# A two-layer kernel on one core: x loaded first, the first gates ahead of the ternary pieces, and the second layer's statistics and inputs moved into the end of the first stage

## The chip, the cores and the metric

One core of one Trainium2 chip. The metric is the device time of one execution in microseconds (us), the median of several runs.

## The reference, cut to what matters

```python
x = L0_attn_x                                   # [2, 512, 256] f32
xn = _layernorm(x)
x = x + _L0_attn_ref(xn, ...) + _L0_ffn_ref(xn, ...)   # gated delta rule, 16 key heads, 32 value heads; ternary SiLU FFN
xn = _layernorm(x)
x = x + _L1_attn_ref(xn, ...) + _L1_ffn_ref(xn, ...)   # attention with 8 experts; GELU FFN, weights -1/0/1 by a threshold
```

In `_L0_attn_ref`, `x @ W_ba` gives beta = sigmoid(b) and g = -exp(A_log) * softplus(a + dt_bias); the products q, k, v go through a four-tap convolution and SiLU, and a rule over chunks of 64 tokens with decays exp(g_i - g_j). `_L0_ffn_ref` rounds its weights to bf16, makes them ternary in groups of 64, and divides the hidden values by their root mean square. `_L1_ffn_ref` compares its weights with 0.7 of their mean magnitude. `_L1_attn_ref` begins with an RMS norm with a weight, the q, k, v products and rotary tables.

## The kernel before, in words

The kernel has four stages with a barrier of all engines between them (`stage_end`, whose waits have line 63): `gdn` (the whole first layer), `layer1_in` (second layer: norm, q, k, v, rotation, and the second FFN's hidden values), `attention` and `experts`.

**The order of the work** in `gdn` is written out by hand. Every engine merges small generators; each yields a due time before a piece of work, and `in_order` issues the pieces by due time, sequentially on the engine. The 16 key heads are turns, 69.84 us apart (`TURN`), and turn 0 has a table of its own, `FIRST`, the last turn `FINAL`; `START` holds the due times of what is done once. Due times set only the order: an engine blocks at a piece whose semaphore isn't there yet, with all that is queued behind it.

**The start.** SyncE's queue issues, by `START`: the first weights `wqk` (2 DMAs, L491), one ternary input A (1 MB, L1176), x (2 DMAs of 512 KB into `yacc`, L174), wv, wz, wo (L496 to L505), then the other two ternary inputs (vn, og). `prep` makes constants, the statistics of x and xn on VectorE (L217 to L228), turns xn tile by tile on TensorE (L272) through two PSUM banks, ScalarE copies each tile out (L308, two copies per tile), and TensorE multiplies by W_ba (L278). VectorE and ScalarE then make the gates (L237 to L261; an Exp, a Ln and a Sigmoid, which each have an activation table of their own), which go to DRAM and back as rows GL and GR (L180, L482). From these TensorE makes the exponents of the decays (L559), ScalarE their exponentials E (L800), and GpSimd multiplies E by a factor `nsk` per token (L1129); VectorE multiplies the key scores by it into CM (L985), CM goes to DRAM and back, and VectorE begins the inverse (L1029).

**The ternary pieces** of the first FFN are six groups g of 128 x 1024: ScalarE casts to bf16 (`act_cast`, L1184), takes the magnitude (L1197) and the sign (L1203); VectorE sums by 64 (L1212) and compares (L1217); GpSimd does four operations (L1227 to L1235); TensorE turns the result (L1247), ScalarE copies it and writes it to DRAM.

**The end of stage one.** Turn 15 lies beside the first FFN: 16 hidden pieces, high and low parts of each for the down product (L1427, L1434), the down product on TensorE (L1388, four token tiles for each half b of the tokens). Between the halves stand 16 one-column products, which sum the squares (L1377), and TensorE waits for VectorE to read them (L1477). The four pieces of the second FFN's weights are compared (L1297, L1302) into one bf16 tile, so each compare waits until TensorE has turned the one before (L1318); ScalarE copies each and writes it to DRAM (L1327 to L1332). VectorE adds the down product to `yacc` at the very end (L1483).

**Stage two** (`layer1_in`) loads its weights and tables on SyncE and ScalarE after the barrier, makes statistics (L1584, L1588), GpSimd the inverse root (L1758), VectorE xn (L1594), TensorE turns xn through two banks (L1537) and multiplies by `wqkv` (L1702), which GpSimd has first scaled by the norm's weight (L1762). VectorE's rotation (L1605) waits for tables that GpSimd scales (L1774) after the DMAs. The hidden products (L1691) wait for parts of x from GpSimd (L1778, L1781); ScalarE's Gelu is L1679.

## Time and profile before

| what | value |
|---|---|
| median of 3 runs | 1536.25 us (1524.79 to 1536.82) |
| the profiled execution | 1536.63 us, span 1534.9 us |
| TensorE busy | 1378.7 us (90%) |
| VectorE, ScalarE, GpSimd busy | 69%, 57%, 35% |
| first stage ends, second begins | 1246.5 us |
| mean granted clock of TensorE | 0.962 |

The page cuts the span into 40 slices of 38.4 us. A timeline gives the start of each operation in us from the span's start, its duration, engine, line and operation, and in brackets how long its engine had been idle and what ended that. "<-issue" means that nothing in the profile explains the wait. L-numbers are lines of the kernel before. Several like instructions in a row are one line, with their count after "x" and their whole time.

### The profile page before, as it was taken

The page shows a single profiled execution, that of the slowest core. Times are in us where ns is not written, and L with a number is a line of the kernel's source. Part 1 is how long each engine was busy: PE and PEld are TensorE (multiplying, and loading weights), DVE is VectorE, ACT ScalarE, POOL GpSimd, SP SyncE. Part 2 cuts the span into 40 slices and gives each one's busy share as a digit, 9 for nine tenths or more (in the row PEclk, how much of TensorE's full clock was granted, in tenths as well). Part 3 has the DMA queues.
Part 4 walks back from the last instruction along what each step waited for, and adds up shares of the span by engine and source line. Part 5 has one row for each costly group of instructions (what it writes and reads, how often), then busy time and mean ns, then how long its engine had stood idle before and what let it go on. Part 6 is the DMA issues. An engine that isn't in the chain of part 4 may idle for free. (4 is left out here: it accounts for less than half of the span.)

```text
span 1534.9 us, 35737 instructions
## 1 busy us (share of the span) xinstructions
PE 1378.7 (90%) x13996; PEld 1033.7 (67%) x13996; DVE 1060.9 (69%) x2152; ACT 867.5 (57%) x1752; POOL 530.0 (35%) x562
## 2 busy tenths in 40 slices
PE   4468999989989999998999999999899967898998
PEld 3236677676777777686777768777678845555755
DVE  3877686848677686867778686877855757774344
ACT  4645666656566666665566666666455616676210
POOL 1772333323323233332323233332345536541000
PEclk9778999999999999999999999999999979899899
DMA  5112110211021012102111120210122040002000
GB/s 170 34 39 59 24 33 22 43 40 26 16 40 30 12 32 64 26 16 39 27 15 32 51 39 16 40 29 13 32 90 69 7 126 1 1 1 60 24 14 14
DMA packets 142486, 56.39 MB, mean 37 GB/s; under 512 B 109776, under 2 KB 134992, under 8 KB 142064
## 3 DMA queue, kind: packets, MB, share of 16 engines
q1 hardware_dynamic: 133424, 48.20, 13.7%
q10 hardware_dynamic: 8896, 5.91, 1.3%
q8 instruction: 113, 1.85, 0.5%
q14 instruction: 53, 0.43, 0.1%
HBM read 37.11 MB, written 16.97 MB: 35 GB/s over the span
## 5 line engine op out<-in xcount | busy, mean ns | idle before, releaser
L1157 POOL TENSOR_TENSOR og<-og,sz 128x256 f32<-128x256 f32 x128 | 94.2, 736 | 512.9 <-DVE og L1100 296.0
L694 PE MATMUL banks<-wz,xT 128*128 128x256 f32 x512 | 128.0, 392 | 10.2 <-DVE yacc L1120 10.2
L947 DVE SCALAR_TENSOR_TENSOR Yv<-banks,cwall,Yv 128x511 f32<-128x511 f32 (+2 forms) x192 | 130.2, 740 | 6.6 <-ACT Yv L787 6.5
L546 PE MATMUL banks<-wv,xT 128*128 128x512 f32 x256 | 119.2, 608 | 11.1 <-DVE Yv L947 9.7
L765 PE MATMUL banks<-wo,oT 128*128 128x256 f32 x512 | 128.0, 394 | 1.1 <-ACT oT L939 1.1
L546 PE MATMUL banks<-wqk,xT 128*128 128x512 f32 x256 | 122.8, 615 | 0.2 <-DVE Yk L947 0.2
L694 PEld LDWEIGHTS banks<-wz,xT 128*128 128x128 f32 x512 | 94.8, 193 | 32.7 <-issue 20.6
L934 ACT ACTIVATE junk<-og 128x512 f32<-128x512 f32 x64 | 40.6, 634 | 117.0 <-POOL og L1157 117.0
L1164 POOL TENSOR_TENSOR rn<-ss,c_half 128x4 f32<-128x4 f32 x64 | 64.9, 1013 | 120.3 <-DVE ss L1114 120.3
L765 PEld LDWEIGHTS banks<-wo,oT 128*128 128x128 f32 x512 | 94.9, 195 | 14.6 <-ACT oT L939 1.4
L738 PE MATMUL banks<-V,A 128*128 128x128 f32 x512 | 84.3, 287 | 9.1 <-ACT V L914 9.1
L546 PEld LDWEIGHTS banks<-wv,xT 128*128 128x128 f32 x256 | 47.3, 196 | 58.9 <-issue 58.7
L1129 POOL TENSOR_TENSOR E<-E,nsk 128x1024 f32<-128x1024 f32 x32 | 60.0, 1897 | 67.7 <-DVE nsk L974 49.2
L1111 DVE TENSOR_REDUCE ss<-junk 128x4 f32<-128x512 f32 x64 | 43.8, 684 | 56.0 <-ACT junk L934 56.0
L738 PEld LDWEIGHTS banks<-V,A 128*128 128x128 f32 x512 | 70.3, 191 | 17.5 <-ACT V L914 13.5
L1086 DVE TENSOR_TENSOR St<-Sd,banks 128x256 f32<-128x256 f32 x64 | 26.9, 420 | 77.3 <-PE banks L743 76.7
L546 PEld LDWEIGHTS banks<-wqk,xT 128*128 128x128 f32 x256 | 48.6, 198 | 43.6 <-issue 42.1
L939 ACT ACTIVATE oT<-banks,nw 128x512 f32<-128x512 f32 x64 | 44.5, 695 | 56.0 <-PE banks L757 55.8
L914 ACT COPY V<-banks 128x256 f32<-128x256 f32 x128 | 47.6, 372 | 42.3 <-PE banks L725 42.2
L725 PEld LDWEIGHTS banks<-R,UB 128*128 128x128 f32 x384 | 55.9, 193 | 20.3 <-issue 12.4
L947 DVE SCALAR_TENSOR_TENSOR Yk<-banks,cwall,Yk 128x511 f32<-128x511 f32 (+2 forms) x96 | 64.5, 740 | 7.1 <-ACT Yk L787 7.0
L1168 POOL TENSOR_TENSOR og<-og,rn 128x512 f32<-128x512 f32 x64 | 67.0, 1047 | 5.0
(412 smaller groups left out, 3658.5 us busy)
## 6 DMA issues: line engine op xcount, KB each, us to landing
cm_d<-CM SPq DMA_DIRECT2D x32, 256.0 KB, 3.9
wqk<-in_L_attn_W_qkvz SPq DMA_DIRECT2D x8, 512.0 KB, 4.4
wv<-in_L_attn_W_qkvz SPq DMA_DIRECT2D x8, 512.0 KB, 4.7
wz<-in_L_attn_W_qkvz SPq DMA_DIRECT2D x16, 256.0 KB, 2.8
wo<-in_L_attn_W_out SPq DMA_DIRECT2D x16, 256.0 KB, 3.1
blk<-cm_d SPq DMA_DIRECT2D x128, 16.0 KB, 1.8
t_d<-tb SPq DMA_DIRECT2D x16, 128.0 KB, 1.7
Td<-t_d SPq DMA_DIRECT2D x128, 16.0 KB, 1.8
```

The source lines that it names most:

```text
L546: ins = pe.matmul(bank[b][:, :], xT[:, d, b * S + of_batch, :], w[:, d, :], start=(d == 0), stop=(d == KD - 1))
L694: ins = pe.matmul(bank[7][:, b * 256:(b + 1) * 256], xT[:, d, b * S + q, :], wz[:, d, :], start=(d == 0), stop=(d == KD - 1))
L725: ins = pe.matmul(pV[:, h * DH:(h + 1) * DH], UB[k % 2][:, h * NT + n, :], R[b][:, h, :] if q else vn[k % 2][:, n, h, :], start=True, stop ...
L738: ins = pe.matmul(pK[:, h * DH:(h + 1) * DH], A[k % 2][:, h, n, :], V0[b][:, h, :], start=True, stop=True)
L765: ins = pe.matmul(bank[7][:, b * D:(b + 1) * D], oT[:, b, h, :], wo[k % 2][:, h, :], start=(h == 0), stop=(h == VR - 1))
L914: act.copy(V0[b][:, :, :], bank[6][:, 0:256].rearrange("p (h d) -> p h d", h=VR)).then_inc(s["V0"].sem, 1)
L939: act.activation(oT[:, :, :, :], bank[7][:, :].rearrange("p (b h t) -> p b h t", b=B, h=VR), ACT.Copy, scale=m["nw"][:, 0:1]).then_inc(s[" ...
L947: v.scalar_tensor_tensor(y, bank[b][:, 0:T - j], conv_w(k, t)[:, 3 - j:4 - j], y, ALU.mult, ALU.add).then_inc(s["tap"].sem, 1)
L1129: pool.tensor_tensor(E[:, h, :, :], E[:, h, :, :], nsk[:, h, :].unsqueeze(2).to_broadcast([P, NT, P]), ALU.mult).then_inc(s["nE"].sem, 1)
L1157: pool.tensor_tensor(og[:, n, :, :], og[:, n, :, :], sz[q % 2][:, b, :].rearrange("p (h d) -> p h d", h=VR), ALU.mult).then_inc(s["osz"].s ...
L1164: pool.tensor_tensor(rn[:, q, :, :], ss[:, q, :, :], c["neghalf"][:, 0:B * VR].rearrange("p (b h) -> p b h", b=B), ALU.pow).then_inc(s["rn ...
L1168: pool.tensor_tensor(o, o, rn[:, q, :, :].unsqueeze(3).to_broadcast([P, B, VR, DH]), ALU.mult).then_inc(s["ogn"].sem, 1)
```

## The change

- **Queue at the start.** x is issued before wqk and A (`START["x"]` -358.07 to -390.0).
- **prep.** The turned tiles go through four banks (0, 1, 4, 5) instead of two, and TensorE's product for tile n comes after the turn of tile n + 4; ScalarE copies a tile in one instruction. The Sigmoid moves ahead of Exp and Ln (due -24.5, -24.4, -24.3), all of them directly after the tile copies.
- **Ternary pieces.** ScalarE's casts: groups 0 and 1 before the tile copies, with their magnitudes (due -25.93 and -24.98); groups 2 and 3 after the gates' Ln; group 4 after the decays' exponentials, group 5 after the squares and copies of the turned keys that follow them (31 later in due time). Magnitudes of groups 2 to 5 come 13.73 later in due time (`qm` -26.73 to -13.0), signs 2.38 later, except that of group 0, which comes right after Ln. On VectorE groups 0 and 1 are summed and compared before the gates; the sum of group 2 is due 9.0 later, at 19.59, the compares of groups 2 and 3 at 31 and 32 (before: 20.4 and 20.9). The norm of the keys (`nk`) stays at 30.53. On GpSimd group 0 begins only when the gates' parts exist, and the factor on E (`nE0`, `nE1`) is due at 24.5 instead of 28.57, which is before the third and fourth operation of group 1 (25.23, 27.23).
- **End of stage one.** The second FFN's compares have tiles of their own (four outputs, two scratch) and come earlier (due 169.5, 175.1, 176.9, 188.0; before 181.13 and on, 4.0 apart), the turns at 185, 186.5, 188.6, 193.5 among the down product, the copies after them. The sums of squares are taken by halves into bank 6: half 0 before the down product, half 1 after its third tile. VectorE adds and takes statistics by halves. SyncE loads wqkv, the norm weight, the rotary tables and b1 when the last turn's key tiles are read (15 DMAs), into `Yq[1]` and two tiles that outlive the stage; GpSimd scales wqkv there, and takes the inverse root for half 0.
- **Stage two.** No statistics, no load of wqkv; the inverse root of half 1 only; four banks for the turned tiles; all other loads on SyncE, with the two FFN weights first, none on ScalarE.

The diff, cut to its core:

```diff
@@ -263,19 +265,19 @@
-        for n in range(NT + 2):
-            if n >= 2:
-                pe.wait_ge(*s["pxT"](n - 2))
+        for n in range(NT + 4):
+            if n >= 4:
+                pe.wait_ge(*s["pxT"](n - 4))
...
-                    ins = pe.transpose(bank[n % 2][:, k * P:(k + 1) * P], xn[:, n, k * P:(k + 1) * P], c["ident"][:, :])
+                    ins = pe.transpose(bank[(0, 1, 4, 5)[n % 4]][:, k * P:(k + 1) * P], xn[:, n, k * P:(k + 1) * P], c["ident"][:, :])
...
-            if n == 2:
+            if n == 4:
...
-            if n >= 2:
+            if n >= 4:
...
-                    ins = pe.matmul(bank[2][:, (n - 2) * 64:(n - 1) * 64], xT[:, k, n - 2, :], wba[:, k, :], start=(k == 0), stop=(k == KD - 1))
+                    ins = pe.matmul(bank[2][:, (n - 4) * 64:(n - 3) * 64], xT[:, k, n - 4, :], wba[:, k, :], start=(k == 0), stop=(k == KD - 1))
@@ -304,9 +306,10 @@
-            for k in range(KD):
-                ins = act.copy(xT[:, k, n, :], bank[n % 2][:, k * P:(k + 1) * P])
-            ins.then_inc(s["pxT"].sem, 1)
+            act.copy(xT[:, :, n, :], bank[(0, 1, 4, 5)[n % 4]][:, 0:D].rearrange("p (k t) -> p k t", k=KD)).then_inc(s["pxT"].sem, 1)
+        yield START["abeta"]
+        act.wait_ge(*s["pgate"](0))
+        act.activation(tab[:, :, BETA, :, :], ba[:, :, 0:VR, :], ACT.Sigmoid).then_inc(s["pact"].sem, 1)
@@ -1179,7 +1193,7 @@
-            yield START["qc"] + g
+            yield START["qc"] + g + (0.0 if g < 2 else 1.0 if g < 4 else 31.0)
@@ -1192,7 +1206,7 @@
-            yield START["qm"] + GROUPS[g] if g else START["q0m"]
+            yield START["qm"] + GROUPS[g] if g > 1 else START["q0m"] + 0.95 * g
@@ -1207,13 +1221,13 @@
-                yield START["qr"] + GROUPS[g] if g else START["q0r"]
+                yield START["qr"] + GROUPS[g] + 9.0 * (g == 2) if g > 1 else START["q0r"]
...
-                yield START["qr"] + GROUPS[2 * i + 1] + 0.5 + 0.5 * (g % 2)
+                yield START["q0r"] + 1.0 if g < 2 else 31.0 + g % 2 if g < 4 else START["qr"] + GROUPS[2 * i + 1] + 0.5 + 0.5 * (g % 2)
@@ -1222,14 +1236,14 @@
+            if g == 0:
+                pool.wait_ge(*s["pgp"](4))
...
-            if g == 0:
-                pool.wait_ge(*s["pgp"](4))
@@ -1274,6 +1288,28 @@
+    def sp_ahead(sp):
+        yield SECOND["load"]
+        sp.wait_ge(*s["KSp"](5, LAST))
+        for name, c0, c1 in (("w_q", 0, D), ("w_k", D, D + KVH * HD), ("w_v", D + KVH * HD, D + 2 * KVH * HD)):
+            sp.dma_start(wqkv[:, :, c0:c1], a["L1_attn_" + name].rearrange("(k p) n -> p k n", p=P)).then_inc(s["l1w"].sem, 16)
+        for k in range(KD):
+            sp.dma_start(an[:, k:k + 1], a["L1_attn_attn_norm_w"][k * P:(k + 1) * P].rearrange("(p o) -> p o", o=1)).then_inc(s["l1an"].sem, 16)
+        for table, name in zip(ropes, ("rope_cos", "rope_sin")):
+            sp.dma_start(table, a[name].rearrange("(q p) e -> p q e", p=P)).then_inc(s["l1c"].sem, 16)
+        for f in range(FF // P):
+            sp.dma_start(b1[:, f:f + 1], a["L1_ffn_b1"][f * P:(f + 1) * P].rearrange("(p o) -> p o", o=1)).then_inc(s["l1b"].sem, 16)
+        sp.wait_ge(*s["l1c"]())
+        sp.wait_ge(*s["l1b"]())
...
+    def pool_ahead(pool):
+        for k in range(KD):
+            yield START["f0"] + FSTEP * (17.5 + k)
+            if k == 0:
+                pool.wait_ge(*s["l1w"]())
+                pool.wait_ge(*s["l1an"]())
+            pool.tensor_scalar(wqkv[:, k, :], wqkv[:, k, :], an[:, k:k + 1], None, ALU.mult).then_inc(s["wq"].sem, 1)
@@ -1291,15 +1327,13 @@
-            i = (g - 6) // 2
-            yield START["q1c"] + 4.0 * (g - 6)
-            v.wait_ge(*(s["qcmp"](g - 1) if g > 6 else s["thr1"](2)))
-            v.tensor_scalar(low1, raw1[g - 6], s2[:, 2 + i:3 + i], None, ALU.is_le).then_inc(s["qlow"].sem, 1)
-            yield START["q1c"] + 4.0 * (g - 6) + 1.0
+            i, lo, out = (g - 6) // 2, low1[g % 2], tern1[g - 6]
+            yield SECOND["low"][g - 6]
+            v.wait_ge(*(s["qcmp"](g - 2) if g > 7 else s["thr1"](2)))
+            v.tensor_scalar(lo, raw1[g - 6], s2[:, 2 + i:3 + i], None, ALU.is_le).then_inc(s["qlow"].sem, 1)
+            yield SECOND["low"][g - 6] + 0.1
...
-            if g > 6:
-                v.wait_ge(*s["qtp"](g - 1))
-            v.scalar_tensor_tensor(tern1, raw1[g - 6], s2[:, i:i + 1], low1, ALU.is_ge, ALU.subtract).then_inc(s["qcmp"].sem, 1)
+            v.scalar_tensor_tensor(out, raw1[g - 6], s2[:, i:i + 1], lo, ALU.is_ge, ALU.subtract).then_inc(s["qcmp"].sem, 1)
@@ -1315,15 +1349,15 @@
-                ins = pe.transpose(bank[4 + g % 2].bitcast(BF16)[:, u * P:(u + 1) * P], tern1[:, at * P:(at + 1) * P], c["identb"][:, :])
+                ins = pe.transpose(bank[4 + g % 2].bitcast(BF16)[:, u * P:(u + 1) * P], tern1[g - 6][:, at * P:(at + 1) * P], c["identb"][:, :])
...
-            yield START["q1e"] + 4.0 * (g - 6)
+            yield SECOND["keep"][g - 6]
...
-            act.wait_ge(*out(g // 2 - 1))
+            act.wait_ge(*out(2))
@@ -1370,13 +1406,12 @@
-            if b:
-                yield START["f0"] + FSTEP * 17
-                pe.wait_ge(*s["f0acc"]())
-                for t in range(TT):
-                    ins = pe.matmul(bank[2][:, t:t + 1], f0acc[t // QT][:, t % QT * P:(t % QT + 1) * P], c["ones"][:, 0:1], start=True, stop=True)
-                ins.then_inc(s["f0ss"].sem, 1)
-                pe.wait_ge(*s["f0ms"]())
+            yield START["f0"] + FSTEP * (16.4 if b == 0 else 17)
+            pe.wait_ge(*s["f0acc"](6 + 7 * b))
+            pe.wait_ge(*(s["f0ms"](0) if b else s["thr1"](0)))
+            for t in range(QT):
+                ins = pe.matmul(sums_at(b)[:, t:t + 1], f0acc[b][:, t * P:(t + 1) * P], c["ones"][:, 0:1], start=True, stop=True)
+            ins.then_inc(s["f0ss"].sem, 1)
@@ -1455,9 +1490,12 @@
-        yield START["f0"] + FSTEP * 18
-        pool.wait_ge(*s["f0ms"]())
-        pool.tensor_tensor(rt[:, :], rt[:, :], c["neghalf"][:, 0:TT], ALU.pow).then_inc(s["f0r"].sem, 1)
+        for b in range(B):
+            yield START["f0"] + FSTEP * (17 + 2 * b)
+            pool.wait_ge(*s["f0ms"](b))
+            pool.tensor_tensor(rt[:, b * QT:(b + 1) * QT], rt[:, b * QT:(b + 1) * QT], c["neghalf"][:, 0:QT], ALU.pow).then_inc(s["f0r"].sem, 1)
+        pool.wait_ge(*s["va"](0))
+        pool.tensor_tensor(rs[:, 0:QT], rs[:, 0:QT], c["neghalf"][:, 0:QT], ALU.pow).then_inc(s["rs"].sem, 1)
@@ -1472,24 +1510,39 @@
-        yield START["f0"] + FSTEP * 17
-        v.wait_ge(*s["f0ss"]())
-        v.tensor_scalar(rt[:, :], bank[2][:, 0:TT], 1.0 / FF, float(np.finfo(np.float32).eps), ALU.mult, ALU.add).then_inc(s["f0ms"].sem, 1)
...
-        v.wait_ge(*s["f0r"]())
...
-        for t in range(TT):
-            v.wait_ge(*s["f0dn"](t // 2))
-            v.scalar_tensor_tensor(yacc[:, t, :], bank[t // 2][:, t % 2 * D:(t % 2 + 1) * D], rt[:, t:t + 1], yacc[:, t, :], ALU.mult, ALU.add).then_inc(s["f0y"].sem, 1)
+        for b in range(B):
+            v.wait_ge(*s["f0r"](b))
+            for i in range(2):
+                v.wait_ge(*s["f0dn"](2 * b + i))
+                for t in (b * QT + 2 * i, b * QT + 2 * i + 1):
+                    v.scalar_tensor_tensor(yacc[:, t, :], bank[t // 2][:, t % 2 * D:(t % 2 + 1) * D], rt[:, t:t + 1], yacc[:, t, :], ALU.mult, ALU.add).then_inc(s["f0y"].sem, 1)
+                v.wait_ge(*s["f0y"](b * QT + 2 * i + 1))
+                for t in (b * QT + 2 * i, b * QT + 2 * i + 1):
+                    ins = v.bn_stats(bn[:, t, :], yacc[:, t, :])
+            ins.then_inc(s["st"].sem, 1)
+            v.wait_ge(*s["st"](b))
+            for t in range(b * QT, (b + 1) * QT):
+                ins = v.bn_aggr(mv[:, t, :], bn[:, t, :])
+            ins.then_inc(s["ag"].sem, 1)
+            v.wait_ge(*s["ag"](b))
+            v.tensor_scalar(rs[:, b * QT:(b + 1) * QT], mv[:, b * QT:(b + 1) * QT, 1], LN_EPS, None, ALU.add).then_inc(s["va"].sem, 1)
...
+    def v_factors(v):
+        for b in range(B):
+            yield SECOND["ms"][b]
+            v.wait_ge(*s["f0ss"](b))
+            v.tensor_scalar(rt[:, b * QT:(b + 1) * QT], sums_at(b), 1.0 / FF, float(np.finfo(np.float32).eps), ALU.mult, ALU.add).then_inc(s["f0ms"].sem, 1)
...
-        streams(sp, (sp_rows, sp_weights, sp_blocks), (start["sp"], sp_ternary), (sp_forward, sp_second))
+        streams(sp, (sp_rows, sp_weights, sp_blocks), (start["sp"], sp_ternary), (sp_forward, sp_second, sp_ahead))
...
-        streams(v, (v_key, v_query, v_value, v_inverse, v_recur, v_finish), (start["v"], v_units, v_ternary), (v_forward, v_down_parts, v_second))
+        streams(v, (v_key, v_query, v_value, v_inverse, v_recur, v_finish), (start["v"], v_units, v_ternary), (v_forward, v_down_parts, v_factors, v_second))
@@ -1569,32 +1621,27 @@
-        for name, c0, c1 in (("w_q", 0, D), ("w_k", D, D + KVH * HD), ("w_v", D + KVH * HD, D + 2 * KVH * HD)):
-            sp.dma_start(wqkv[:, :, c0:c1], a["L1_attn_" + name].rearrange("(k p) n -> p k n", p=P)).then_inc(s["l1w"].sem, 16)
...
-        for f in range(FF // P):
-            sp.dma_start(b1[:, f:f + 1], a["L1_ffn_b1"][f * P:(f + 1) * P].rearrange("(p o) -> p o", o=1)).then_inc(s["l1b"].sem, 16)
+        for k in range(KD):
+            sp.dma_start(mn[:, k:k + 1], a["L1_attn_moe_norm_w"][k * P:(k + 1) * P].rearrange("(p o) -> p o", o=1)).then_inc(s["l1s"].sem, 16)
+        sp.dma_start(b2[:, :], a["L1_ffn_b2"].partition_broadcast(P)).then_inc(s["l1s"].sem, 16)
+        sp.dma_start(gw[:, :, :], a["L1_attn_gate_w"].rearrange("(k p) n -> p k n", p=P)).then_inc(s["l1gw"].sem, 16)
+        sp.dma_start(wo[:, :, :], a["L1_attn_w_o"].rearrange("(k p) n -> p k n", p=P)).then_inc(s["l1wo"].sem, 16)
+        sp.wait_ge(*s["l1s"]())
...
-        sp.wait_ge(*s["l1b"]())
...
-            ins = v.bn_stats(bn[:, t, :], xa[:, t, :])
-        ins.then_inc(s["st"].sem, 1)
-        v.wait_ge(*s["st"]())
-        for t in range(TT):
-            ins = v.bn_aggr(mv[:, t, :], bn[:, t, :])
-        ins.then_inc(s["ag"].sem, 1)
-        v.wait_ge(*s["ag"]())
-        v.tensor_scalar(rs[:, 0:TT], mv[:, :, 1], LN_EPS, None, ALU.add).then_inc(s["va"].sem, 1)
-        v.wait_ge(*s["rs"]())
-        for t in range(TT):
+            if t == QT:
+                v.wait_ge(*s["rs"]())
...
-        v.tensor_tensor(r8[:, :], mv[:, :, 1], rs[:, 0:TT], ALU.mult).then_inc(s["ms"].sem, 1)
-        v.wait_ge(*s["ms"](0))
-        v.tensor_tensor(r8[:, :], r8[:, :], rs[:, 0:TT], ALU.mult).then_inc(s["ms"].sem, 1)
+            if t == QT:
+                v.tensor_tensor(r8[:, :], mv[:, :, 1], rs[:, 0:TT], ALU.mult).then_inc(s["ms"].sem, 1)
+            elif t == QT + 1:
+                v.wait_ge(*s["ms"](0))
+                v.tensor_tensor(r8[:, :], r8[:, :], rs[:, 0:TT], ALU.mult).then_inc(s["ms"].sem, 1)
@@ -1705,7 +1741,11 @@
-            pe_turned(pe, s, "xTt", c, bank, xn, t, "xTe")
+            if t >= 4:
+                pe.wait_ge(*s["xTe"](t - 4))
+            for k in range(KD):
+                ins = pe.transpose(over(t)[:, k * P:(k + 1) * P], xn[:, t, k * P:(k + 1) * P], c["ident"][:, :])
+            ins.then_inc(s["xTt"].sem, 1)
@@ -1753,15 +1793,9 @@
+        pool.tensor_tensor(rs[:, QT:TT], rs[:, QT:TT], c["neghalf"][:, QT:TT], ALU.pow).then_inc(s["rs"].sem, 1)
...
-        pool.wait_ge(*s["va"]())
-        pool.tensor_tensor(rs[:, 0:TT], rs[:, 0:TT], c["neghalf"][:, 0:TT], ALU.pow).then_inc(s["rs"].sem, 1)
-        pool.wait_ge(*s["l1w"]())
-        pool.wait_ge(*s["l1an"]())
-        for k in range(KD):
-            pool.tensor_scalar(wqkv[:, k, :], wqkv[:, k, :], an[:, k:k + 1], None, ALU.mult).then_inc(s["wq"].sem, 1)
...
-        pool.wait_ge(*s["l1s"]())
```

## Rows read from the trace of the kernel before

**Rows 1.** part 2 of the page: busy tenths of TensorE and its granted clock, 40 slices of 38.4 us

```profile
PE   4468999989989999998999999999899967898998
...
PEclk9778999999999999999999999999999979899899
```

**Rows 2.** timeline, all engines, first 55 us (start, duration, engine, line, operation, [idle before, releaser])

```profile
12.34 1.04 ACT L1184 CAST Yk<-A 128x1024 bf16<-128x1024 f32 x1 [7.03 <-DMA A<-in_L_ffn_w_gate_up]
...
15.39 2.71 DVE L217 BATCH_NORM_STATS2 bn<-yacc 128x6 f32<-128x256 f32 x8 [10.37 <-DMA yacc<-in_L_attn_x]
...
21.31 1.88 PE L272 MATMUL banks<-c_ident,E 128*128 128x128 f32 x6 [21.31 <-DVE E L228]
...
28.85 2.66 PE L278 MATMUL banks<-Td,xT 128*128 128x64 f32 x12
...
32.63 0.41 DVE L237 TENSOR_TENSOR CM<-banks,Td 128x256 f32<-128x256 f32 x1
...
50.02 0.61 PE L559 MATMUL banks<-c_later,c_identb 128*128 128x512 bf16 x1 [8.28 <-DMA GR<-g_d]
...
54.07 1.09 ACT L800 ACTIVATE E<-banks 128x512 f32<-128x512 f32 x2
```

**Rows 3.** source view of L491, the first two weight loads: time from issue to landing

```profile
DMA to landing us min/median/max: 4.1/4.8/5.6
```

**Rows 4.** source view of L1217, VectorE's compares: duration in ns, min/median/max

```profile
L1217 DVE TENSOR_TENSOR A<-A,qthr x2: 1218/1222/1227, 44.5 to 45.7; 128x1024 bf16<-128x1024 bf16 x2
L1217 DVE TENSOR_TENSOR vn<-vn,qthr x2: 2912/2970/3029, 55.5 to 58.5; 128x1024 bf16<-128x1024 bf16 x2
```

**Rows 5.** timeline of VectorE, first turn

```profile
46.82 1.21 DVE L1212 TENSOR_REDUCE qsum<-vn 128x16 f32<-128x1024 bf16 x1
...
65.66 0.17 DVE L974 TENSOR_SCALAR nsk<-sk 128x16 f32<-128x16 f32 x1
...
69.82 1.22 DVE L985 TENSOR_TENSOR CM<-banks,E 128x1024 f32<-128x1024 f32 x1 [0.60 <-POOL E L1129]
...
82.94 0.37 DVE L1029 TENSOR_TENSOR t<-blk,tb 128x2 f32<-128x2 f32 x1
```

**Rows 6.** timeline of GpSimd, first turn

```profile
45.85 3.03 POOL L1227 TENSOR_TENSOR A<-A 128x1024 bf16<-128x1024 bf16 x1 [18.83 <-DVE A L1217]
...
65.97 3.75 POOL L1129 TENSOR_TENSOR E<-E,nsk 128x1024 f32<-128x1024 f32 x2 [0.37 <-POOL Yk L1235]
```

**Rows 7.** timeline of TensorE, one projection in turn 0, one in turn 1

```profile
98.86 6.72 PE L546 MATMUL banks<-wv,xT 128*128 128x512 f32 x8 [9.68 <-DVE Yv L947]
...
151.54 3.60 PE L546 MATMUL banks<-wv,xT 128*128 128x512 f32 x8
```

**Rows 8.** timeline of the end of stage one and its barrier, all engines

```profile
1218.41 0.47 PE L1388 MATMUL banks<-f_down,f_x_hi 128*128 128x256 f32 x1
...
1229.93 0.39 PE L1388 MATMUL banks<-f_down,f_gate 128*128 128x256 f32 x1 [1.32 <-DVE f_r L1477]
...
1238.55 1.28 DVE L1302 SCALAR_TENSOR_TENSOR Yq<-kt,q_s,Yq 128x1024 bf16<-128x1024 f32 x1 [2.93 <-PE banks L1318]
...
1239.76 3.22 DVE L1483 SCALAR_TENSOR_TENSOR yacc<-banks,f_r,yacc 128x256 f32<-128x256 f32 x8
...
1241.94 0.52 ACTq L1332 DMA_DIRECT2D down_d<-kt  x1
1246.52 0.95 POOL L1756 MEMSET vp<- 128x1024 f32 x1 [14.43 <-POOLq L63]
```

**Rows 9.** timeline of the opening of stage two, all engines

```profile
1252.64 2.33 PE L1537 MATMUL banks<-c_ident,l_xn 128*128 128x128 f32 x8 [11.77 <-DVE l_xn L1594]
...
1254.76 4.77 PE L1702 MATMUL banks<-wqkv,xT 128*128 128x384 f32 x8
...
1265.11 7.09 PE L1702 MATMUL banks<-wqkv,xT 128*128 128x384 f32 x16 [2.13 <-ACT vp L1651]
...
1274.69 1.27 ACT L1679 ACTIVATE h<-banks,b 128x512 f32<-128x512 f32 x2
```

57 lines of the change are left out of this document (27 added, 30 removed), and 8 rows, old and new, of tables (FIRST, START).

## Prediction

> **What bounds the kernel now.** I read the page's slices first. The reader is to see TensorE at 9 tenths from the fifth slice to the last, and at 4, 4, 6 and 8 tenths in the first four, where its granted clock falls too [rows 1]. Between the two ends of stage one TensorE is the bound, so whatever brings its full turns forward moves the whole rest, and nothing that the change does to the other engines in between counts. So the second view is the timeline of the first 83 us, and the third that of the end of stage one and the opening of stage two, where TensorE stands idle for 11.8 us: it ends its last turns at 1240.9 (the ScalarE copy before the issue at 1241.94 takes 1.0) and starts again at 1252.64 [rows 8, 9].
>
> The start is a chain. x lands at 15.39, A earlier, at 12.34; TensorE turns x and makes the gate product from 21.31 to 31.51, VectorE begins the gates at 32.63, the decays reach TensorE at 50.02 and ScalarE at 54.07 [rows 2]. The factor `nsk` is ready at 65.8, CM at 71.04, the inverse begins at 82.94 [rows 5].
>
> **Part 1, the start.** x at the front of the queue takes the place of wqk, whose two loads landed 4.1 and 5.6 us after their issue [rows 3]; with pieces half as long I put x at 7.5 instead of 15.39. Statistics, root and xn then keep their length (21.31 - 15.39 = 5.9), so TensorE turns the first four tiles from 13.4. But ScalarE's queue now has two casts and two magnitudes of A ahead of the tile copies, and A goes from second to third place: it lands between 12.34 and 15.39, where the second and third place land now [rows 2]. I take 14.5, then four operations of 1.04, 18.6. So the copies start 3.1 before TensorE's start of today plus a copy's delay (21.31 + 0.7), and TensorE has half of the turns behind it. Its eight tiles took 10.2 us; with four turned, about 8.5 are left: 27.1 instead of 31.5. The gates begin at 28.4, that is 4.2 earlier (bounds: 2.5 if A takes until 15.39 and little is saved on tiles, 6 if it lands at 12.34).
>
> Gates to decays took 50.02 - 32.63 = 17.4. Two ternary magnitudes that stood among them are gone (1.0 each), one compare group's sum too (1.21 [rows 5]), but the three activation tables are still loaded one after the other, so I count 0.7: decays at 45.1, 4.9 earlier.
>
> From the decays to CM I add what is now in each queue. ScalarE has the second magnitude and first sign ahead of the exponentials, so these start 2.7 after the decays instead of 4.05. `nsk` gets rid of two compares in front of it, which took 2.97 each [rows 4]; it gets the sum of group 3, due at 19.91, which waits for a magnitude queued behind two late casts and the key copies: 3 times 1.04 on ScalarE and 1.21 on VectorE, some 4.5 with the scales. Together: `nsk` at 60.2 instead of 65.8. GpSimd is ready for its product with E long before: group 0 can begin some 6 ahead of the decays, at 39, and with operations of 2 to 3 us (3.03 is the slowest [rows 6]) six of them end at about 52; there it stands until 60.2, since the product is next in its order (before, it began at 65.97 right behind group 1 [rows 6]). Behind `nsk` on VectorE stand two compares beside a GpSimd product: 2.4 us at the unhindered 1.22 each, 5.9 at 2.97 each [rows 4], I take 4.0; a sum, 1.2; CM, 2.4. CM ends at 67.9 instead of 71.04: 3.1 earlier. The query's taps, its scores and the inverse follow as they do now, so turn 0 and all behind it gain **3.1 us**. Bounds: 5.5 with free compares and an early A; -3 if GpSimd's wait of some 8 passes on through groups 1 and 2 to the memset of the inverse's tile, which stands behind them.
>
> The Trainium skill ("SBUF — State Buffer", section "Who interferes with whom") says that a VectorE instruction with two SBUF inputs contends with a GpSimd instruction that reads SBUF, and that the one that comes later blocks for the whole of the other. By that rule both compares would wait a GpSimd product out and the start would gain about 1.2; the trace has both cases, 1.22 and 2.97 [rows 4].
>
> **Part 2, the end of stage one.** TensorE's down product starts at 1218.41. Removed: its wait of 1.32 for the sums [rows 8], and the stretch at the lower clock level right behind that wait, about 2 us. Added: compare 7 now stands ahead of hidden piece 14 on VectorE (0.74 and 1.28, as the compares at the end [rows 8]), and the down product waits for that piece: 1.1 us. TensorE ends at 1238.4, 2.5 earlier. Behind it now comes VectorE: two additions at 0.40 (eight take 3.22 [rows 8]), two statistics at 0.34 (eight take 2.71 [rows 2]), and small sums and waits, which I estimate at 0.9: 2.4 us. Today the stage ends by a copy, a DMA issued at 1241.94 and the barrier, until 1246.52; the last turn is now two tiles of product earlier, so the DMA is down before VectorE is. VectorE at 1240.8, drain and barrier 1.6, the next stage at 1242.4 to 1243. Gain **3.7** (bounds 2 and 5). SyncE's 15 issues stand in front of nothing but the stage's last waits. GpSimd's product with wqkv comes where GpSimd is idle beside the down product; it is two operations, smaller than the 1.9 of its 128 x 1024 ones [rows 6], so uncovered it would cost under 3.8.
>
> **Part 3, the opening.** TensorE starts 6.12 behind the barrier (1252.64 - 1246.52); with the statistics gone it starts 0.8 behind it. Then its work is the same: from 1252.64 to the end of the last product at 1272.20 are 19.6, the first product at 4.77 in it, less the wait of 2.13 for the rotation [rows 9]. That wait hung on the DMAs and on GpSimd's tables; its chain is now a root, two memsets, a second root and four small products, which I estimate at 6.2 from the barrier, and the third product is asked for at 11. So the products end at 18.2 behind the barrier. ScalarE's first Gelu, which paces the rest, starts at 28.17 behind it (1274.69), with a table load in front; now, a hidden product and two hand-overs behind 18.2, at 20.0, the load done while it waits. What follows hangs on ScalarE. I take 7.6, between TensorE's 7.5 and ScalarE's 8.2 (the upper bound); the lower is 6, if GpSimd's parts of x (L1781), which begin at the last tile's copy, come last.
>
> **The sum.** 3.1 + 3.7 + 7.6 = 14.4. The profiled execution took 1536.63, 0.4 above the median: 1522.2, and I say **1522**.
>
> **The rivals.**
> *A, the start gives nothing.* x may land no earlier than A in practice, or ScalarE's order (copies behind A) and GpSimd's wait for `nsk` take back what x gives; the four magnitudes of 1.04 and the 8 us wait speak for it, the 5.9 of compares that leave the path against it. 1536.6 - 11.3 = 1525.
>
> *B, the clock.* In turn 0 a projection takes 6.72 that takes 3.60 in turn 1 [rows 7]; the granted clock is at its lower level in parts of slices 2 to 4 [rows 1], after TensorE had waited. If shorter waits keep it at the upper level, two such projections and the query scores give back 3.1, 2.7 and 2: 1514. Against it: the waits there are VectorE's and stay.
>
> *C, slower.* The same mechanism the other way: turns 0 and 1 have about 20 us of TensorE work at the upper level between 60 and 160 us. If waits in the new order (the GpSimd and VectorE stops above) drop the clock for all of it, that costs 20, and from 14.4 on it eats the whole gain: 1542. For it: the level moves several times there already. Against it: none of the new waits is TensorE's own.
>
> **How the numbers follow.** Forecast 0.53, with its own range 1517 to 1528; A 0.22; B 0.18; C 0.07. The range is 1511 to 1533: it takes in A and most of B, and the sum of the low ends (-3 + 2 + 6 = 5, 1532) and of the high ones (5.5 + 5 + 8.2 = 18.7, 1518) with the clock on top. A measurement here can tell about 1% from no change, 15.4 us, so 1521 is the edge, 1 us under my forecast: of the forecast's 0.53 I give 0.24 to faster, B whole: 0.42. Slower by 1% is most of C: 0.05. The rest, 0.53, is within 1%.
>
> **What would show it.** Right: x in VectorE at 7 to 8 and the first tile copy on ScalarE at 18 to 20; gates at about 28, decays at 45, GpSimd idle before the product with E, CM done at 66 to 70, the full turns about 3 earlier; the second stage from 1237 to 1242 (1246.5 less 3.1 and 3.7 is 1239.7); TensorE 0.8 behind it, the first Gelu 20 behind it. Wrong: CM at 71 or later (the first term falls), a TensorE wait for compares or high and low parts in the down product, VectorE not the last before the barrier, or a Gelu that starts earlier with no gain in what comes after it.

## The result and the profile after

| | before | after |
|---|---|---|
| median, 20 runs each | 1536.03 us | 1522.53 us |
| lowest and highest | 1524.79 to 1543.29 | 1516.76 to 1534.45 |
| profiled execution, span | 1536.63, 1534.9 | 1528.98, 1527.2 |

The ratio is 0.9923, 95% interval [0.9904, 0.9942]; a second measurement of the same kernel, in other rounds, gave 0.9939 [0.9907, 0.9971]. So the change is worth some 9 to 12 us. The ratios here and below leave out two executions, one of 3458 us of `start_alone` and one of 1550 us of the kernel before. The number forecast, 1522, lies on the first median, but the two profiled executions differ by only 7.7 us, and they don't split it as the prediction did. The same marks in both traces:

| mark, us from the span's start | before | after | gained so far |
|---|---|---|---|
| factor `nsk` of turn 0 | 65.66 | 60.04 | 5.6 |
| CM done | 71.04 | 67.78 | 3.3 |
| first inverse begins | 82.94 | 80.21 | 2.7 |
| first inverse ends, value's taps begin | 95.33 | 95.52 | -0.2 |
| factor of turn 1 | 138.13 | 137.22 | 0.9 |
| factor of turn 15 | 1088.23 | 1088.93 | -0.7 |
| stage two's first VectorE instruction | 1246.56 | 1245.59 | 1.0 |
| first hidden product of stage two | 1271.74 | 1264.03 | 7.7 |
| last DMA issue (the output) ends | 1531.84 | 1524.22 | 7.6 |

The slices of the page answer to [rows 1]: TensorE reaches 9 tenths in the fifth slice as before.

```profile
PE   4568999999989999999999899999999987898998
...
PEclk9578999999999999999999999999999999999999
```

The start, from the timeline of the kernel after, answers to [rows 2] and [rows 5]. x is there at 7.59, the tile copies start at 19.54, the gates at 29.36, the decays at 45.65; `nsk` is ready at 60.21, two compares take 4.05 beside GpSimd's product, CM ends at 67.78.

```profile
7.59 2.71 DVE L219 BATCH_NORM_STATS2 bn<-yacc 128x6 f32<-128x256 f32 x8 [2.58 <-DMA yacc<-in_L_attn_x]
...
15.47 1.05 ACT L1198 CAST Yk<-A 128x1024 bf16<-128x1024 f32 x1 [10.35 <-DMA A<-in_L_ffn_w_gate_up]
...
19.54 0.63 ACT L309 COPY xT<-banks 128x256 f32<-128x256 f32 x2
...
29.36 0.41 DVE L239 TENSOR_TENSOR CM<-banks,Td 128x256 f32<-128x256 f32 x1
...
45.65 0.61 PE L573 MATMUL banks<-c_later,c_identb 128*128 128x512 bf16 x1 [8.36 <-DMA GR<-g_d]
...
60.04 0.17 DVE L988 TENSOR_SCALAR nsk<-sk 128x16 f32<-128x16 f32 x1
...
60.20 4.05 DVE L1231 TENSOR_TENSOR vn<-vn,qthr 128x1024 bf16<-128x1024 bf16 x2
60.34 5.67 POOL L1143 TENSOR_TENSOR E<-E,nsk 128x1024 f32<-128x1024 f32 x2 [7.76 <-issue]
```

Then comes the inverse. Below are its multiplies and the GpSimd instructions beside them, in order of time. The reader is to compare ends: 80.21 + 1.60 is 81.81, and the GpSimd instruction of 79.68 ends at 81.80; 82.04 + 1.98 is 84.02, and the GpSimd instruction of 81.88 ends at 84.00; 84.25 + 1.75 is 86.00, against 85.98; 86.72 + 2.02 is 88.74, against 88.65; 89.01 + 1.96 is 90.97, against 90.84. Five multiplies end when the GpSimd instruction that had begun before them ends; that of 86.25, which begins beside a memset (L1157), takes 0.21.

```profile
79.68 2.12 POOL L1249 TENSOR_TENSOR UB<-UB,vn 128x1024 bf16<-128x1024 bf16 x1
80.21 1.60 DVE L1043 TENSOR_TENSOR t<-blk,tb 128x2 f32<-128x2 f32 x1 [0.83 <-DMA blk<-cm_d]
...
81.88 2.12 POOL L1243 TENSOR_TENSOR vn<-vn 128x1024 bf16<-128x1024 bf16 x1
82.04 1.98 DVE L1043 TENSOR_TENSOR t<-blk,tb 128x8 f32<-128x8 f32 x1
...
84.08 1.90 POOL L1245 TENSOR_TENSOR vn<-vn,qscale 128x1024 bf16<-128x1024 bf16 x1
84.25 1.75 DVE L1043 TENSOR_TENSOR t<-blk,tb 128x18 f32<-128x18 f32 x1
...
86.03 0.53 POOL L1157 MEMSET Td<- 128x512 f32 x1
86.25 0.21 DVE L1043 TENSOR_TENSOR t<-blk,tb 128x32 f32<-128x32 f32 x1
...
86.52 2.13 POOL L1247 TENSOR_TENSOR vn<-vn,UB 128x1024 bf16<-128x1024 bf16 x1
...
86.72 2.02 DVE L1043 TENSOR_TENSOR t<-blk,tb 128x50 f32<-128x50 f32 x1
...
88.72 2.12 POOL L1249 TENSOR_TENSOR UB<-UB,vn 128x1024 bf16<-128x1024 bf16 x1
...
89.01 1.96 DVE L1043 TENSOR_TENSOR t<-blk,tb 128x72 f32<-128x72 f32 x1
...
95.52 4.03 DVE L961 SCALAR_TENSOR_TENSOR Yv<-banks,cwall,Yv 128x511 f32<-128x511 f32 x6
```

In the kernel before, three of the seven multiplies are that long (those of 8, 32 and 50 columns, 5.8 us together); the one of 18 columns between two of them, which begins beside the memset, takes 0.18:

```profile
83.53 1.75 DVE L1029 TENSOR_TENSOR t<-blk,tb 128x8 f32<-128x8 f32 x1
...
85.32 0.52 POOL L1143 MEMSET Td<- 128x512 f32 x1
85.52 0.18 DVE L1029 TENSOR_TENSOR t<-blk,tb 128x18 f32<-128x18 f32 x1
```

The end of stage one answers to [rows 8]. TensorE's wait of 1.32 between the halves of the down product is gone; ahead of the down product stands a new one of 2.01 for hidden piece 14 (L1512), which VectorE makes only at 1221.38, behind ternary piece 7 (L1333, L1336). VectorE is the last before the barrier, as forecast.

```profile
1213.98 1.59 DVE L1333 TENSOR_SCALAR Yq<-UB,q_s 128x1024 bf16<-128x1024 f32 x1
...
1215.60 2.20 DVE L1336 SCALAR_TENSOR_TENSOR UB<-UB,q_s,Yq 128x1024 bf16<-128x1024 f32 x1
...
1219.40 0.74 DVE L1333 TENSOR_SCALAR Yq<-UB,q_s 128x1024 bf16<-128x1024 f32 x1
...
1220.17 1.28 DVE L1336 SCALAR_TENSOR_TENSOR UB<-UB,q_s,Yq 128x1024 bf16<-128x1024 f32 x1
1221.38 0.68 DVE L1512 TENSOR_TENSOR vn<-Yv,banks 128x512 f32<-128x512 f32 x1
...
1222.11 0.39 PE L1423 MATMUL banks<-f_down,f_x_hi 128*128 128x256 f32 x1 [2.01 <-DVE vn L1512]
...
1244.24 0.17 DVE L1530 TENSOR_SCALAR rs<-mv 128x4 f32<-128x4 f32 x1
...
1245.59 3.14 DVE L1639 TENSOR_SCALAR l_xn<-yacc,mv,rs 128x256 f32<-128x256 f32 x5 [1.18 <-PEq L63]
```

The opening of stage two answers to [rows 9]: TensorE starts 0.5 behind the barrier, its first hidden product 18.4 behind it (25.2 before), the first Gelu 20.3 (28.1). The products of `wqkv` (L1738; the tile that holds the weights is called `q_odd` in these rows) take 3.94, 2.75 and 5.40, where before they took 4.77, 2.75 and 7.09, and the first hidden product waits 1.97 for a part of x from GpSimd (`x_lo`, L1815). The stretch's own row (length, then busy time and count of TensorE, its weight loads, VectorE, ScalarE, GpSimd; granted clock, DMA share, GB/s) has the clock at 0.91 (before, from the barrier to the first hidden product: 0.69).

```profile
1248.23 3.94 PE L1738 MATMUL banks<-q_odd,xT 128*128 128x384 f32 x8
...
1256.66 5.40 PE L1738 MATMUL banks<-q_odd,xT 128*128 128x384 f32 x16 [1.03 <-ACT vp L1689]
...
1264.03 0.97 PE L1729 MATMUL banks<-x_hi,l1w1T 128*128 128x512 f32 x2 [1.97 <-POOL x_lo L1815]
...
1265.89 0.69 ACT L1717 ACTIVATE h<-banks,b 128x512 f32<-128x512 f32 x1 [1.53 <-PE banks L1729]
```

```profile
1245.60:1264.00 18.40, 14.36 (x48) 8.38 (x48) 15.52 (x28) 6.42 (x16) 13.66 (x15) 0.91 0.41 137
```

### The profile page after: what moved, and what is told of

It reads as the page before. It is cut to its first block and busy times, and to the rows that moved or that the text cites. A ratio compares the mean times of both kernels' runs of the same rounds, so it can differ in the third digit from the quotient of the medians.

```text
span 1527.2 us, 35728 instructions
## 1 busy us (share of the span) xinstructions
PE 1379.8 (90%) x13996; PEld 1034.0 (68%) x13996; DVE 1062.8 (70%) x2154; ACT 869.5 (57%) x1745; POOL 534.7 (35%) x564
## 5 line engine op out<-in xcount | busy, mean ns | idle before, releaser
L752 PEld LDWEIGHTS banks<-V,A 128*128 128x128 f32 x512 | 69.9, 191 | 17.7 <-ACT V L928 13.7
```

Of the source, the lines that this page charges most:

```text
L752: ins = pe.matmul(pK[:, h * DH:(h + 1) * DH], A[k % 2][:, h, n, :], V0[b][:, h, :], start=True, stop=True)
```

## The experiments

Every kernel ran in rounds beside the kernel before; ratios are to it. Single executions of one kernel differ by up to 23 us (why, is the fourth question), so a claim about one step rests on its marks in the trace, and the ratio only says whether it contradicts them.

### One: is the start worth 3.1 us?

`start_alone`: the kernel before with the start's edits only.

```diff
-    "x": -358.07, ... "abeta": -4.67, ... "asp": -4.67, ... "asp2": -4.67,
+    "x": -390.0, ... "abeta": -24.5, ... "asp": -24.4, ... "asp2": -24.3,
-    "qm": -26.73, "qg": -3.78, "q0m": -25.93, "q0g": -25.84,
+    "qm": -13.0, "qg": -1.4, "q0m": -25.93, "q0g": -24.2,
-    "nE0": 28.57, "nE1": 28.57
+    "nE0": 24.5, "nE1": 24.5
```

with the four banks and the new places of casts, magnitudes and compares.

> The kernel before with the edits of the start alone (x first, gating ahead of the ternary pieces, two compares at once, the two products with E moved up). Theory given-back: the gates come some 3 us earlier and CM ends near 68, but VectorE's inverse, which then lies beside four more GpSimd pieces, ends at 95 to 96 as before (95.33); the key factor of turn 1 comes 0 to 1.5 us earlier than 138.1, and the time is 0 to 1.5 us under the kernel before, which five rounds can't tell from nothing. Theory passed-on (the prediction's term): the inverse ends near 92, turn 1 comes 3 us earlier and the time is 3.1 us under.

Measured: 1.0019 [0.9994, 1.0044]. `nsk` at 60.25, CM done at 68.00, the inverse from 80.28 to 95.72. Its first multiply, one of the five that stall (9.4 us together), and the taps behind it:

```profile
80.28 1.74 DVE L1028 TENSOR_TENSOR t<-blk,tb 128x2 f32<-128x2 f32 x1 [1.07 <-DMA blk<-cm_d]
...
95.72 4.03 DVE L946 SCALAR_TENSOR_TENSOR Yv<-banks,cwall,Yv 128x511 f32<-128x511 f32 x6
```

`start_undone`, the kernel after with the same edits taken back:

> The kernel after with the start put back, the end of stage one and the opening of stage two kept. Theory given-back: 12 to 13 us under the kernel before, within 1.5 us of the changed kernel. Theory passed-on: 10.4 us under, 3.1 slower than the changed kernel. In both its opening (barrier to first hidden product) takes 18.5 us as in the changed kernel, 25.2 before.

Measured: 0.9941 [0.9917, 0.9966], between 5 and 13 us under before, an interval that holds both theories' numbers; its inverse ends at 95.48. What decides is the other run and the marks. A start that passed on 3.1 us would have a ratio of 0.998, and `start_alone` lies above that with its whole interval. And the first inverse ends at 95.3 and 95.5 in the two traces with the old start, at 94.8 to 95.7 in the seven with the new start and five stalled multiplies (`start_alone`, both traces of the changed kernel, and four more runs below). The factor of turn 1 stands at 138.1 and 137.1 in the two, at 135.7 to 138.3, 137.1 in the mean, in the seven: a gain of 0.5, which the scatter hides.

`factor_behind` moves one thing in the kernel after: the product with E goes back behind the last two GpSimd pieces of group 1, which fill most of GpSimd's idle 7.76 us (3.35 are left).

```diff
-"nE0": 24.5, "nE1": 24.5
+"nE0": 28.57, "nE1": 28.57
```

> The kernel after with the two products with E put back behind the last two GpSimd pieces of group 1, which so fill GpSimd's idle 7.76 us ahead of the products. Theory given-back by collision: GpSimd's pieces of groups 2 and 3 run 4.2 us earlier and end near 86.6 and not 90.8; of the five small multiplies of the inverse that last 1.6 to 2.0 us about two become 0.2 to 0.3 us; the inverse ends near 92 and not 95.5, turn 1 comes some 3.5 us earlier (key factor at 133.7 and not 137.2) and the time is 3 to 3.5 us under the changed kernel. Rival: the multiplies are slow for a reason of their own (they wait for the inverse's data), then the inverse ends at 95.5 and nothing is gained.

Measured: 0.9918 [0.9892, 0.9943]; inverse 78.56 to 91.70, factor of turn 1 at 132.17. Four multiplies still stall, 6.9 us together, and end with a GpSimd instruction (two below: 82.31 + 2.06 against 82.17 + 2.12, 84.62 + 1.97 against 84.37 + 2.12); those behind them take 0.28 and 0.33. The inverse ends where the theory had it (92), and turn 1 comes 1.5 earlier than it had (133.7); the 3 us can't be read in the ratio, since the intervals overlap. TensorE's clock was also granted in full for more of this turn, so of the 5.0 us at turn 1 only the 3.8 of the inverse are put down to the edit.

```profile
82.17 2.12 POOL L1247 TENSOR_TENSOR vn<-vn,UB 128x1024 bf16<-128x1024 bf16 x1
...
82.31 2.06 DVE L1043 TENSOR_TENSOR t<-blk,tb 128x32 f32<-128x32 f32 x1
...
84.37 2.12 POOL L1249 TENSOR_TENSOR UB<-UB,vn 128x1024 bf16<-128x1024 bf16 x1
...
84.62 1.97 DVE L1043 TENSOR_TENSOR t<-blk,tb 128x50 f32<-128x50 f32 x1
```

`group_three_behind` adds a wait, so that no GpSimd piece lies beside the inverse:

```diff
-            then = START["qp"] + GROUPS[g]
+            then = START["qp"] + GROUPS[g] if g != 3 else 55.0
...
+            if g == 3:
+                pool.wait_ge(*s["sub"](17, 0))
```

> As factor_behind, and GpSimd's four pieces of group 3 (8.3 us) wait for the last reduction of the first inverse. Theory collision: no GpSimd product lies beside the inverse's small multiplies, each lasts 0.2 to 0.4 us, the inverse takes 7.1 us as in turn 1 and ends near 86; the taps behind it then wait for ScalarE's copy of the next projection (87.5 in factor_behind), start near 87, and the key factor of turn 1 comes near 128 (132.2 in factor_behind): 4 to 4.6 us under factor_behind, 8 under the changed kernel (before its clock differences). Rival: the GpSimd pieces moved behind it make group 3, and with it groups 4 and 5, late, TensorE waits for their turned pieces, and what the inverse gains is given back before turn 1: key factor at 131 to 134.

Measured: 0.9923 [0.989, 0.9957], no better as a whole than `factor_behind`; but the mechanism is bare here:

```profile
79.40 0.15 DVE L1043 TENSOR_TENSOR t<-blk,tb 128x2 f32<-128x2 f32 x1
...
86.49 2.12 POOL L1245 TENSOR_TENSOR vn<-vn 128x1024 bf16<-128x1024 bf16 x1 [6.93 <-DVE tb L1049]
...
87.69 4.03 DVE L961 SCALAR_TENSOR_TENSOR Yv<-banks,cwall,Yv 128x511 f32<-128x511 f32 x6 [1.28 <-ACT Yv L801]
```

The seven multiplies take 0.15 to 0.32 us, the inverse 7.0 (79.40 to 86.41) and not 15.3 (so it does, to 0.01, in the three later kernels that have this wait), and the taps then wait 1.28 for ScalarE, at 87.69. That is 4.0 earlier than in `factor_behind`; by turn 1 (130.35 against 132.17) 1.8 are left, where the theory had 4 to 4.6, so both the theory and its rival hold in part. (In the three later kernels turn 1 comes at 129.6 to 131.1, so this mark is good to 1 us.) GpSimd's groups 4 and 5 come 2.0 earlier than in `factor_behind` and TensorE makes the next projection at a lower clock (6.64 for eight products, behind its wait of 3.87; 5.41 in `factor_behind`). Behind that projection 2.8 of the 4.0 are left, so part of the loss lies there and the rest behind it; neither was tried by itself.

### Two: what bounds the end of stage one?

`piece_behind`, in the kernel after:

```diff
-SECOND = {"low": (169.5, 175.1, 176.9, 188.0), ...
+SECOND = {"low": (169.5, 175.4, 176.9, 188.0), ...
```

> The kernel after with the second ternary piece of layer two behind the product of hidden piece 14 on VectorE and not ahead of it. Theory new-wait: TensorE's wait of 2.0 us ahead of the down product for that product goes; the down product starts 2 us earlier against the last hidden piece, the second stage begins 2 us earlier and the time is 2 us under the changed kernel. Rival: the next thing (the parts of the last hidden pieces, or the turned pieces) is late in its place, the wait moves inside the down product, and nothing is gained.

`two_pieces_behind` has (169.5, 175.4, 182.7, 188.0):

> As piece_behind, and the third ternary piece of layer two behind the product of hidden piece 15 as well. In piece_behind TensorE's wait of 2.0 us ahead of the down product had turned into one of 1.5 us for GpSimd's second sum of squares. Theory VectorE's order: with both pieces behind, the product of piece 15 comes 2 us earlier, the sum with it, both waits are gone, and from the key factor of the last turn to the barrier it takes 152.5 to 153.5 us where TensorE's clock is full (154.8 in factor_behind, whose clock was full). Rival: VectorE's whole queue bounds the end of the stage, the remainders of the parts (L1469) then come late and TensorE waits for them: 154.8 again.

Measured: 0.9948 [0.992, 0.9977] and 0.9944 [0.9909, 0.9978]. Both theories failed: the wait moved each time. In order, TensorE in `piece_behind`, then in `two_pieces_behind`:

```profile
1239.15 1.02 PE L1413 MATMUL banks<-c_ones,Td 128*128 128x1 f32 x7 [1.50 <-POOL Td L1492]
```

```profile
1224.46 1.63 PE L1413 MATMUL banks<-c_ones,Td 128*128 128x1 f32 x8 [1.65 <-DVE f_r L1536]
```

2.01 for a hidden piece, then 1.50 for GpSimd's sum of squares, then 1.65 for the factor on VectorE, which its order puts behind the remainders. `factor_early` (with the other edits below) takes that one as well:

```diff
-"ms": (184.2, 187.0)
+"ms": (177.5, 187.0)
```

> all_weights_later with VectorE's first factor of the sum of squares (L1540, 4 columns) put behind the second ternary piece and ahead of the remainders of the parts. In all_weights_later and two_pieces_behind TensorE waited 1.6 us inside the down product for that instruction alone. Theory VectorE's order, third try: the wait goes and no other takes its place, no half clock follows it, and from the last turn's key factor to the barrier it takes 152.5 to 153.5 us (154.7 to 155.1 in the others, each less half of what it had at half clock); the time is 1.5 to 2 us under all_weights_later. Rival: the stage's end is bounded by VectorE's queue as a whole, which every order leaves as long as it is, and 154.5 to 155 comes out again.

Measured: 0.9842 [0.9801, 0.9883]. No wait over 0.3 us is left in the down product, but VectorE then ends 2.9 us behind TensorE and not 2.3. From the last turn's factor to the barrier, less half of the time at the lower clock level (a rough correction, since TensorE isn't busy all that time), the kernel before takes 155.9 and `start_alone`, whose end is the same, 154.9; the kernel after takes 155.0 and 154.5 in its two traces, `piece_behind` 155.5, `two_pieces_behind` 154.7, `factor_early` 154.5, `factor_behind` and `weights_later`, with the clock full throughout, 154.8 and 155.1. None came near 153: no order of VectorE's queue that was tried is worth 1 us, as the rival has it. That the queue's whole length is the bound isn't tested by an order; `stats_in_stage_two`, in the third question, makes the queue shorter and gets to 153.1.

### Three: what opened stage two earlier?

`stats_in_stage_two` puts layer two's statistics back behind the barrier and keeps the loads and the scaled weights ahead of it.

```diff
-                for t in (b * QT + 2 * i, b * QT + 2 * i + 1):
-                    ins = v.bn_stats(bn[:, t, :], yacc[:, t, :])
...
+        for t in range(TT):
+            ins = v.bn_stats(bn[:, t, :], xa[:, t, :])
```

> The kernel after with layer two's statistics put back behind the barrier, the early loads and the scaled weights kept. Theory statistics: TensorE's first instruction comes 6 us behind the barrier again and not 0.5, the first hidden product 23.5 to 24 and not 18.5, the barrier itself comes 1.4 us earlier since VectorE's tail lacks them, and the time is some 4 us over the changed kernel. Rival weights: the loads and the scaling were what held the projections; then the late statistics cost little, the hidden product comes 19 to 20 behind the barrier, and the time is the changed kernel's.

Measured: 0.9936 [0.9905, 0.9968]. In its trace TensorE starts 5.8 behind the barrier, the first hidden product 23.5 (25.2 before, 18.4 after); from the last factor to the barrier it takes 153.1, clock counted as above, 1.9 less than the kernel after. So of the 6.7 us that the opening gained in these traces, 5.1 are the statistics' and 1.7 the loads' and weights', and the statistics cost 1.9 of it in stage one. The split is rough: before the first hidden product the opening takes 27.7 and not 25.2 in `start_alone`, whose stage two is that of the kernel before, and 17.1 to 19.1 in the eleven traces with the new one. The ratio can't separate the net 3.2 us from nothing.

### Four: why do runs of one kernel differ by some 20 us?

The turns 2 to 14 last 65.8 to 74.0 us, and in every trace the long ones have a stall in the middle of the inverse's first 128 products of 32 x 32 (L615), "<-issue". Turn 5 of the kernel after, its TensorE and SyncE rows, and the DMA queues from 442 to 444:

```profile
439.71 0.45 SPq L510 DMA_DIRECT2D wv<-in_L_attn_W_qkvz  x1
...
441.42 1.10 PE L615 MATMUL banks<-Td,CM 32*32 32x32 f32 x106
...
445.15 0.54 PE L615 MATMUL banks<-Td,CM 32*32 32x32 f32 x22 [2.63 <-issue]
```

```profile
q1 hardware_dynamic: 165, 0.31, 40.0%
q8 instruction: 1, 0.02, 3.0%
```

106 of 128 products are done at 442.52, then TensorE stands 2.63 us; in that stretch one packet of the instruction queue (16 KB) arrives amid the 512 KB weight load issued at 439.71. It is no accident of this turn: in the fourteen traces the turns 2 to 14 have 73 such stalls of 1.2 us and more, and every one ends 2.2 to 2.8 us behind the start of such a packet. From 445.1 to 448.5 the clock granted is 0.50, the lower of its two levels, 1.2 GHz. `weights_later` holds these loads until the 128 products are done.

```diff
             if k:
                 sp.wait_ge(*s["proj"](3, k - 1))
+                sp.wait_ge(*s["P16p"](0, k - 1))
...
             if k:
                 sp.wait_ge(*s["proj"](7, k - 1))
+                sp.wait_ge(*s["P16p"](0, k - 1))
```

> The kernel after with the loads of the next weights (512 KB each, three in every fourth turn, one in every other second) held until TensorE has finished the first 128 small products of the turn's inverse. Theory of the scatter: in the ten traces at hand those products stall in mid-course, 1.2 to 4.9 us, for TensorE's own instructions, whose load shares the DMA engines with these weights, most in turn 3 with three loads, and a stall of some 2.4 us and more is followed by 3.4 to 6.8 us at half clock. So here no such stall in a turn with loads is over 1.6 us, turns 2 to 14 together have at most 7 us at half clock (17.1 in the changed kernel), and the time is 5 to 9 us under the changed kernel, with less scatter. Rival: the instructions' load is slow by itself, or the later weights hold up the projection that needs them (3.6 us of it 10 us after), and nothing is gained.

`after_again` is the changed kernel beside it:

> The changed kernel itself, beside these two on one chip, with a second trace. Theory: its first inverse ends at 95.3 to 95.7 again, TensorE waits 2.0 us ahead of the down product again, stage two's first hidden product comes 18.5 us behind the barrier, and 10 to 13 us under the kernel before. If the start's gain had been lost by chance in the first trace, the inverse would end at 92 to 93 here.

Measured: `weights_later` 0.9907 [0.9879, 0.9935], `after_again` 0.9939 [0.9907, 0.9971]; the inverse of `after_again` ends at 94.83, half a microsecond under the expectation, from a chain that began that much earlier (59.35); its wait of 2.0 and its opening of 18.6 are as expected, and by its ratio it lies 9.4 us under the kernel before, a little less than the 10 to 13 expected. Turn 3 has three such loads; first `after_again`, then `weights_later`:

```profile
304.07 0.96 SPq L505 DMA_DIRECT2D wqk<-in_L_attn_W_qkvz  x2
...
305.80 1.14 PE L615 MATMUL banks<-Td,CM 32*32 32x32 f32 x110
...
310.90 0.52 PE L615 MATMUL banks<-Td,CM 32*32 32x32 f32 x18 [3.96 <-issue]
```

```profile
305.32 1.29 PE L617 MATMUL banks<-Td,CM 32*32 32x32 f32 x128 [0.90 <-DMA Td<-t_d]
...
306.69 0.90 SPq L506 DMA_DIRECT2D wqk<-in_L_attn_W_qkvz  x2
```

The turn takes 72.6 us in the one and 67.2 in the other. The longest stall is 3.0 to 4.8 us in each of the eleven traces whose loads aren't held, 1.9 in `weights_later`, 1.7 in `all_weights_later`, 1.8 in `factor_early`. In the eleven, the stalls of the odd turns, which load wv or wqk, take 2.4 to 4.8 us and those of the even turns 1.2 to 2.2; with the loads held all take 1.4 to 1.9. So the loads lengthen the stall and don't make it. The stalls of 1.4 to 1.9 stay, over the 1.6 expected, and some are followed by a stretch at 1.2 GHz, so the expected "at most 7 us at half clock" was a miss (13.7 here in turns 2 to 14, as in the first trace of the changed kernel), and the ratio alone doesn't separate it from `after_again`.

### Five: a kernel that beats both

`all_behind` is `group_three_behind` with `two_pieces_behind`, `all_weights_later` adds `weights_later`.

> The edits of group_three_behind and of two_pieces_behind together. If both theories hold their gains add: 8 us from the start and 1.5 to 2 us from the end of stage one, some 10 us under the changed kernel: 1512 to 1513 us, ratio to the kernel before 0.985. If both rivals hold it is 1518 to 1523.

> all_behind and weights_later together. Theory: 8 us from the start, up to 2 from the end of stage one and 5 to 9 from the turns, 1504 to 1510 us, ratio to the kernel before 0.980 to 0.984. Rival: as in weights_later, 1512 to 1518.

Measured: `all_behind` 0.9888 [0.9835, 0.9941], with a median of 1520.16 us in the range of the two rivals (1518 to 1523), though the 0.985 expected lies inside the interval; `all_weights_later` 1512.61 us, 0.9856 [0.9811, 0.99], with turns 1 to 14 in 942.7 us (951.7 after), in the rival's range (1512 to 1518) and not in the theory's (1504 to 1510); `factor_early`, which builds on it, 1514.29 us and 0.9842. The intervals of the last two lie below both of the changed kernel: by the ratios some 10 to 15 us faster than it.

## Why the prediction was right or wrong

**The start's chain** was right to the microsecond: x 7.59 (forecast 7.5), A about 15.4 (14.5, the high bound), tile copies 19.5 (18.6), gates 29.4 (28.4), decays 45.7 (45.1), `nsk` 60.0 (60.2), the compares 4.05 (4.0), CM 67.8 (67.9). By that mark the gain was 3.3, forecast 3.1.

**The step that failed** is the sentence behind it: "The query's taps, its scores and the inverse follow as they do now, so turn 0 and all behind it gain 3.1 us." The inverse doesn't follow as it does now. GpSimd's groups 2 and 3 end where they did (90.84, before 90.1), because the product with E, now ahead of the last two operations of group 1, left GpSimd idle for 7.76 us while it waited for `nsk`. An inverse that starts 2.7 earlier so lies beside more of them: five multiplies stall (9.3 us together), three before (5.8). The end stays at 95.5. I had seen the idle and priced it only as a delay passed on to a memset; the price lay in what it pushed beside VectorE. The term is 0 at the inverse's end; at turn 1 it is 0.9 in the first pair of traces and 0.5 between the means of two and seven traces; and the start alone has a ratio of 1.0019. That is rival A's outcome (1525) by a step that A doesn't name: GpSimd's wait does take back what x gives, but by pushing its next pieces beside the inverse; the two measurements, 9.4 and 11.8 us under before, are in the mean nearer to its 1525 (1536.0 less 9.4 and 11.8 is 1526.6 and 1524.2) than to 1522.

The Trainium skill ("SBUF — State Buffer", section "Who interferes with whom") says that a VectorE instruction with two SBUF inputs and a GpSimd instruction that reads SBUF shut each other out, and that the later one blocks fully. The multiplies above show it: both inputs in SBUF, and each ends with the GpSimd instruction; the reductions between them, one input, take 0.16 to 0.26 us throughout, and a multiply beside a memset 0.21. I had weighed the rule for the two compares and not for the small operations, where the instruction shut out is some ten times shorter than the one it waits for.

**The end of stage one**, forecast 3.7, measured 1.7 between the marks of the first pair (158.3 to 156.7 from turn 15's factor to the barrier) and 0.6 with the clock counted and two traces of each. The wait of 1.32 went, as forecast; three things did not come as written. The wait for hidden piece 14, forecast 1.1, was 2.0: ternary piece 6 in front takes 3.8 beside GpSimd's product and additions (1.59 and 2.20, unhindered 0.74 and 1.28, both pairs in the rows above) and holds VectorE's queue up as well. The "stretch at the lower clock level", 2 us, was not removed: it came at 1223.3, behind the new wait. VectorE's tail, 2.3 (forecast 2.4), and the barrier, 1.2 (1.6), were right. The sign that I had named, a TensorE wait for compares inside the down product, isn't there in these words: the wait stands ahead of it, for the piece that the compares hold up. The sum itself was off by 0.3: 1.32 and 2 less 1.1 is 2.2, not 2.5.

**The opening**, forecast 7.6, measured 6.7: TensorE 0.5 behind the barrier (0.8), products and conversions until 18.4 (18.2), first Gelu 20.3 (20.0). The length was right because two errors cancelled. The sum kept the products' old lengths and took off every wait; the trace has products 2.5 shorter (12.1 for 14.6, with TensorE's clock at its upper level for more of them) and waits of 0.6 for xn, 1.0 for ScalarE (`vp`) and 2.0 for GpSimd's `x_lo`. The last is the case that the lower bound, 6, names, GpSimd's parts of x coming last. The term was read at ScalarE's first Gelu (28.1 to 20.3, 7.8), which before stood 3.0 behind the first hidden product and now 1.9, and that 1.1 is not passed on: the hidden products set the pace, 25.2 to 18.4.

**The sum** was 14.4; the terms measured in the first pair add up to 0.9 + 1.7 + 6.7 = 9.3, and 1.6 went the other way in the turns between, by chance. Between the first medians lie 13.5 us, by the two ratios 11.8 and 9.4, so the number was met with luck. More traces shift the shares. From the barrier to the end of the execution it takes 288.3 and 290.7 us with the old stage two and 278.3 to 281.7, 280.1 in the mean, in the eleven traces with the new one: 9.4 us, with 0.5 from the start and 0.6 from the end of stage one 10.5, which is what the ratios say. So the start and the end of stage one gave some 5.7 less than forecast, and stage two 1.8 more. Part of that is the clock: the first stretch at 1.2 GHz lasts until 10.7 and 12.2 us behind the barrier with the old opening, in which TensorE stands idle for the first 6.1, and until 3.6 to 6.4 with the new one. In turns 0 and 1 neither B nor C came: the clock granted in the first 100 us and in the second is 0.78 and 0.90 (0.82 and 0.89 before). B's mechanism, shorter waits that keep the upper level, shows in the opening instead, where the 25 us before had 0.69 and now have 0.86.

**Slips in the working** that changed no forecast by more than 0.3 us where it can be followed: the copies start 3.4, not 3.1, ahead of the mark that it names (22.0 less 18.6). For `nsk` it can't be followed: the changes it lists (4.9, 1.35 and 5.9 off, 4.5 on) lead from 65.8 to 58.1 and not to 60.2. That 60.2 was met (60.0) is therefore no proof of the working; in the trace VectorE waits 9.40 for the magnitude of group 3 ahead of it, the piece that the text names.

## What to carry to other kernels

When a chain starts earlier, ask of each later piece what it will lie beside; a piece of 0.2 us costs 2 us if another engine's long instruction holds the port, and an engine left idle ahead of its work pushes that work onto the next chain. Read a moved wait at the engine that paces the rest, not at the first one that starts earlier. When a wait goes, take the next two in the queue away on paper as well: here three other orders of one queue gave the same end. And when a sum comes out, check its terms: here one was near 0 and another too small, and the total came out.

## What was not expected of the hardware

TensorE stalls at a place in its stream that moves on evenly, behind 112, 106 and 94 of the 128 products in turns 2, 5 and 11, for 1.2 to 4.8 us. I read it as a wait for its own instructions: the place, and the instruction packet ahead of the end of all 73 stalls, speak for it. Those of 3 us and more all lie in turns that load wv or wqk. In fourteen traces, of 182 turns (2 to 14 of each), 109 had no such stall and last 66.8 us in the mean; 15 had one of 3 us or more, every one with a stretch at 1.2 GHz, and last 72.9. The other 58 had a shorter one, 24 of them such a stretch, and last 69.1; of the 109, four had one. The thirteen turns together take 875.7 to 892.9 us in the fourteen traces, and of the 3.3 us between the two traces of the changed kernel 3.0 lie there. That it is most of the scatter between all runs is likely, but only traces show it. The Trainium skill ("Runtime: NRT & Kernel Launch", section "Instruction fetch mechanics") has it that the fetch is hidden behind the issue of instructions; here, with many short products in a row, it is not, by 1.2 to 2.2 us in turns without a weight load and by up to 4.8 beside one, and the measurement decides.
